# Four attentions of one kernel: 18 score tiles ahead of the loop in place of 24, three a step in the first six steps, and another place for the second norm

## What is computed

```python
x = x + _L0_attn_ref(_layernorm(x), ...)   # window and global tokens, ALiBi, rope, 8 key heads   -> stage a0
x = x + _L0_ffn_ref(_layernorm(x), ...)
x = x + _L1_attn_ref(_layernorm(x), ...)   # causal                                            -> stage a1
x = x + _L1_ffn_ref(_layernorm(x), ...)
x = x + _L2_attn_ref(_layernorm(x), ...)   # causal with rope                                  -> stage a2
x = x + _L2_ffn_ref(_layernorm(x), ...)
x = x + _L3_attn_ref(_layernorm(x), ...)   # full, heads mixed over batches                    -> stage a3
x = x + _L3_ffn_ref(_layernorm(x), ...)
```

## Time and profile before

| what | us |
|---|---|
| median of 3 runs | 1944.53 |
| lowest and highest | 1933.18, 1951.77 |
| the profiled execution | 1942.08 |
| its span | 1940.3 |
| PE busy in it | 1628.8 |
| DVE busy in it | 1179.9 |
| ACT busy in it | 865.3 |
| POOL busy in it | 477.8 |

### The profile page before, as it was taken

The page is one execution under the profiler, slowest core; times in us unless marked ns, Lnnn a source line. Parts: engine busy times, 40 slices in busy tenths (PEclk is TensorE's granted clock), DMA queues, the critical chain, the costliest instruction groups (busy, mean ns, idle before and its releaser), DMA issues. The chain is left out here.

```text
span 1940.3 us, 28833 instructions
## 1 busy us (share of the span) xinstructions
PE 1628.8 (84%) x10648; PEld 942.5 (49%) x10654; DVE 1179.9 (61%) x2595; ACT 865.3 (45%) x1360; POOL 477.8 (25%) x594
## 2 busy tenths in 40 slices
PE   4989999899999999911499999869998999998676
PEld 2334443478855556501245555546775344433433
DVE  2677777343255665469857676456454777775476
ACT  1255555433215555522025445437673366566322
POOL 4222210023213312030222330016664422210100
PEclk9789999999999999965699999969999999999798
DMA  7351350100064335010245424031113355140322
GB/s 244 81 130 52 85 135 2 66 1 0 1 182 126 94 87 153 2 50 0 70 124 152 123 64 120 1 123 50 50 50 93 110 126 150 36 120 1 118 88 88
DMA packets 68688, 162.29 MB, mean 84 GB/s; under 512 B 10013, under 2 KB 15526, under 8 KB 67562
## 3 DMA queue, kind: packets, MB, share of 16 engines
q1 hardware_dynamic: 68554, 160.52, 29.2%
HBM read 111.06 MB, written 53.09 MB: 85 GB/s over the span
## 5 line engine op out<-in xcount | busy, mean ns | idle before, releaser
L1079 DVE TENSOR_REDUCE a_mx<-PS 128x1 f32<-128x512 f32 (+3 forms) x768 | 395.0, 553 | 184.3 <-PE PS L1321 113.0
L1262 ACT ACTIVATE a_pT<-PS 128x1024 f32<-128x1024 f32 (+3 forms) x384 | 308.6, 811 | 222.4 <-PE PS L1345 154.5
L1316 PE MATMUL PS<-a_k,a_q 64*128 64x512 f32 (+3 forms) x768 | 228.6, 413 | 30.4 <-DVE a_mx L1079 24.5
L405 DVE CUSTOM_DVE_ANT_0 PS<-PS,a_dist 128x448 f32<-128x448 f32 x256 | 156.2, 642 | 59.6 <-PE PS L650 58.3
L1336 PE MATMUL PS<-a_q,a_k 64*128 64x512 f32 (+3 forms) x768 | 174.2, 433 | 6.2 <-issue 3.2
L1359 PE MATMUL PS<-a_pT,a_va 128*32 128x512 f32 (+3 forms) x1536 | 166.8, 506 | 5.7 <-ACT a_raw L1220 5.7
L122 PE MATMUL PS<-cst 128*128 128x512 f32 x248 | 131.1, 657 | 44.5 <-PEq L66 35.2
L555 ACT ACTIVATE a_pT<-PS 128x448 f32<-128x448 f32 (+1 forms) x256 | 123.5, 542 | 95.4 <-PE PS L673 95.0
L1316 PEld LDWEIGHTS PS<-a_k,a_q 64*128 64x128 f32 x768 | 105.7, 186 | 102.6 <-DVE a_mx L1079 87.8
L1336 PEld LDWEIGHTS PS<-a_q,a_k 64*128 64x128 f32 x768 | 77.2, 185 | 107.2 <-issue 78.5
L2046 POOL TENSOR_TENSOR f_h_low<-f_prod,f_h_high 128x512 fp32r<-128x512 f32 x84 | 110.2, 1318 | 60.2 <-ACT f_h_high L2233 57.8
(11 more groups left out here) (355 smaller groups left out, 3449.9 us busy)
## 6 DMA issues: line engine op xcount, KB each, us to landing
spread_scratch<-a_high SPq DMA_DIRECT2D x96, 256.0 KB, 7.3
a_q<-spread_scratch SPq DMA_DIRECT2D x96, 256.0 KB, 5.7
a_k<-spread_scratch SPq DMA_DIRECT2D x96, 256.0 KB, 6.4
f_gb<-gate_rows SPq DMA_DIRECT2D x68, 256.0 KB, 5.2
spread_scratch<-a_low SPq DMA_DIRECT2D x48, 256.0 KB, 7.8
a_q<-window_scratch SPq DMA_DIRECT2D x32, 256.0 KB, 5.4
a_k<-window_scratch SPq DMA_DIRECT2D x32, 256.0 KB, 6.3
window_scratch<-a_high SPq DMA_DIRECT2D x24, 256.0 KB, 3.5
```

What stands on the lines that cost most here:

```text
L405: dve.tensor_tensor_reduce(PS[:, 4 + a, 0:KW], PS[:, 4 + a, 0:KW], dt_[:, off:off + KW], 1.0, 3e38, ALU.add, ALU.min, mx[:, gg % 2, qt, 2 ...
L1079: dve.tensor_reduce(mx[:, gg % 2, qt, 2 * half + a:2 * half + a + 1], PS[:, 4 + a, 0:kw], AX.X, ALU.max).then_inc(max_done, 1)
L1262: act.activation(pT[:, N // 2 % 2, N % 2, :, q0:S], PS[:, 2 * (N % 2):2 * (N % 2) + 2, q0:S], ACT.Exp, scale=SCALE).then_inc(exp_done, 1)
L1316: mm = pe.matmul(ps[:, 0:kw], q[rows, b % 2, pair, qt * P:(qt + 1) * P], k[rows, b % 2, pair, 0:kw], start=True, stop=not causal)
```

## The change

The number of tiles ahead of the loop goes from 24 to 18 in all four attentions. The loop does three tiles in each of steps 0 to 5 and two from then on, so that from step 5 on the same tiles are done as before. `turn_maxima(0, 0)` comes after tile 17 in place of tile 19, with the `keep_busy` of 3 right behind it, and a0 gets that `keep_busy` too. In DVE's list the stats of the second norm go to behind unit 1's exchange where there is rope (in a1 and a3 they stay), and apply, and in a0 `total(1)`, go ahead of tile 0; a0's `sigmoid(1)` goes behind `keep_minima(0, 0)`. In POOL's list the norm's root goes between unit 1 and unit 2.

```diff
-    LEAD = 24
+    FIRST, LEAD = 18, 24
+        def scored(N):
+
+            return min(NB * TILES_, 2 * (N + 1) + LEAD, FIRST + 3 * (N + 1))
+
 (attention_window, POOL)
-                layer_norm_pool(pool, ln, 1, neg_half)
-                pool.wait_ge(ln.rstd_done, 2)
+                    if u == 1:
+                        layer_norm_pool(pool, ln, 1, neg_half)
+                pool.wait_ge(unit_low[NU - 1], 1)
                 pool.memset(pT[GLOB:P, 2, :, GLOB:S], 0.0).then_inc(ones_done, 1)
 (attention_window, DVE)
                     exchange(0, u)
-                layer_norm_stats(dve, ln, 1, source(1))
+                    if u == 1:
+                        layer_norm_stats(dve, ln, 1, source(1))
                 dve.wait_ge(loaded_dist, 16)
-                for t in range(8):
-                    minima(t)
                 dve.wait_ge(transposed, 2 * KC)
                 layer_norm_apply(dve, ln, 1, source(1))
-                for t in range(8, 4 * TB):
+                total(1)
+                for t in range(FIRST):
                     minima(t)
-                total(1)
-                for t in range(4 * TB, LEAD):
-                    minima(t)
+                keep_minima(0, 0)
                 sigmoid(1)
-                keep_minima(0, 0)
                 for N in range(FULL):
-                    for t in (2 * N + LEAD, 2 * N + LEAD + 1):
-                        if t < NB * TILES_:
-                            minima(t)
+                    for t in range(scored(N - 1), scored(N)):
+                        minima(t)
 (attention_window, PE)
-                for t in range(4 * TB + 4):
+                for t in range(FIRST):
                     scores(t)
                     if t % 2:
                         keep_busy(pe, PS, cst, 3, 1)
                 pe.wait_ge(va_done, 1)
                 turn_minima(0, 0)
-                for t in range(4 * TB + 4, LEAD):
-                    scores(t)
+                keep_busy(pe, PS, cst, 3, 3)
                 pe.wait_ge(masks_done, 2)
                 for N in range(FULL):
                     scores_T(N)
-                    for t in (2 * N + LEAD, 2 * N + LEAD + 1):
-                        if t < NB * TILES_:
-                            scores(t)
+                    for t in range(scored(N - 1), scored(N)):
+                        scores(t)
 (attention_quads, POOL)
                 if rope is not None:
-                    for u in range(NU):
+                    for u in range(2):
                         rotated(0, u)
                         lower(0, u)
                 layer_norm_pool(pool, ln, 1, neg_half)
+                if rope is not None:
+                    for u in range(2, NU):
+                        rotated(0, u)
+                        lower(0, u)
 (attention_quads, DVE)
                         exchange(0, u)
+                        if u == 1:
+                            layer_norm_stats(dve, ln, 1, source(1))
                 else:
...
-                layer_norm_stats(dve, ln, 1, source(1))
-                for t in range(4 * TB):
-                    maxima(t)
+                    layer_norm_stats(dve, ln, 1, source(1))
                 dve.wait_ge(transposed, KC)
                 layer_norm_apply(dve, ln, 1, source(1))
-                for t in range(4 * TB, LEAD):
+                for t in range(FIRST):
                     maxima(t)
                 keep_maxima(0, 0)
 (attention_quads, PE)
-                for t in range(4 * TB + 4):
+                for t in range(FIRST):
                     scores(t)
                     if t % 2:
                         keep_busy(pe, PS, cst, 3, 1)
                 pe.wait_ge(va_done, 2)
                 turn_maxima(0, 0)
-                for t in range(4 * TB + 4, LEAD):
-                    scores(t)
                 keep_busy(pe, PS, cst, 3, 3)
```

More of the change, by code:

```diff
@@ L1163, in _ @@
                 for N in range(FULL):
-                    for t in (2 * N + LEAD, 2 * N + LEAD + 1):
-                        if t < NB * TILES_:
-                            maxima(t)
+                    for t in range(scored(N - 1), scored(N)):
+                        maxima(t)
                     piece(*piece_at(N))
```

## The result

The kernel after is slower: 1956.8 us as the median of 16 runs, against 1939.16 for the kernel before on the same chips, a ratio of 1.0075 with a 95% interval of 1.0051 to 1.0100 (the ratio leaves out one slow run of after, at 1967.98, and is that of the means of the others, 1954.7 and 1940.1). The forecast was 1935.0, in a range of 1925 to 1948. The runs of after also scatter more (1935.1 to 1967.98; those of before 1933.18 to 1951.77). Their time goes with the mean granted clock of the whole execution: 1935.1 us at 0.930, the other fifteen 1946.0 to 1967.98 us at 0.923 to 0.909. The profiled execution took 1956.33 us, with a span of 1954.5.

The account below looks back on a forecast made before the run. No one engine bounds the kernel, though PE, 84% busy, leads in the loop's first steps. Gains of 5.0 + 1.8 + 1.7 + 1.0 = 9.5 us give 1932.6 profiled, 1935.0 median, range 1925 to 1948.

Parts of the forecast that it names:

- The entry: Tile 16 to the loop: takes 4.8 us in the new order, so the loops start earlier, together 17.3 us gained.
- The price of the owed tiles: Steps 0 to 5: third tiles wait for DVE, costing 3.8 us in a3, 2.4 in a1, 2.5 in a2, 4.8 in a0.
- the walk: Step-by-step sum of steps 0 to 5 with the old trace's durations; in a3 step 6 came at 14.1 us for 10.26.
- the clock: Rival, loop steps: DVE waits bring one slow stretch of 1.7 us per attention, a0's tiles stay slow; 1944 us, chance 0.2.
- two well-sized terms: The 17.3 us gained ahead of the loops, against the cost of the same 24 tiles issued inside steps 0 to 5.
- Third tiles at full price: Rival, steps 0 to 5: each third tile costs 1.17 us, 28.1 against 17.3 gained; 1955 us, chance 0.17.
- The slack: Rival, steps 0 to 5: the six steps hide the owed tiles, 17.3 to 20 us gained; 1926 us, chance 0.12.
- The norm's move: Second norm's apply (1.4 us) and a0's sum (1.2) go where DVE waits for the spread, costing nothing.
- The fall inside the keep-busy: a0 ahead of tile 0: the clock falls late and briefly after 3.9 us of idle, costing 2 us.
- the signs of "wrong": Profile after: step 6 at its old distance, a0's tiles at 0.70, a new slow stretch in steps 0 to 8, DMA wait.
- signs of "right": Profile after: entry 4.8 us, half-microsecond idle before third tiles, step 6 at 14, 12.8, 16 us, a0's tiles at 1.00.

Follow-up runs that it names:

- the late order: The kernel after with the third tile of steps 0 to 5 moved behind the step's values and piece in PE's list: 0.9970 of before.
- the runs with filler: The kernel after plus a useless 128 x 256 matmul ahead of third tiles: steps 0 to 5 0.9992, 0 and 1 0.9984, 2 to 5 0.9993 of before.
- the late order with filler: The kernel after with third tiles behind values and piece, plus one useless matmul in steps 0 and 1: 0.9954 of before.
- the fastest kernel: The kernel before with only the second norm's move, plus the triple keep-busy ahead of a0's loop: 0.9911 of before.
- the filler: The kernel after plus one useless 128 x 256 matmul, behind a wait for bank 7, ahead of the third tile of steps 0 to 5: 0.9992 of before.
- the twelve steps: The kernel after with the six owed tiles spread over twelve steps, one extra every second step: 1.0068 of before.
- the run without the entry filler: The kernel before with only the second norm's move, less the triple keep-busy before the loop of a1 to a3: 0.9949 of before.
- filler in steps 0 and 1: The kernel after plus the useless 128 x 256 matmul ahead of the third tile in steps 0 and 1 alone: 0.9984 of before.

## Why the prediction was wrong, step by step

- **The entry was right.** Tile 16 to `scores_T(0)` takes 4.5 to 4.6 us (4.8 forecast), and tile 0 to the loop gains 5.7, 4.4, 4.4 and 5.0 in a0 to a3, 19.5 in all, against 2.4 + 17.3 = 19.7 forecast. In a0 it is 5.7 of 6.5, with tiles 0 to 15 at a clock of 0.79 and not at the 1.00 of the forecast.
- **The price of the owed tiles was about right at full clock, and too low in a0.** To step 6 the walk had 2.4 in a1 and 3.8 in a3; to step 8 the late order measured 2.9 and 3.7. For a2 it had 2.5, and the runs with filler have 21.55 - 18.80 = 2.8 and 21.30 - 18.80 = 2.5. For a0 it had 4.8; the late order with filler needs 22.2 to step 8 where the fastest kernel needs 17.3: 4.9. The sum is 14.3 against the 13.5 of the walk. The plain order without any filler never ran wholly at full clock in a1 to a3, so its own price stays bracketed: in a1 between 2.7 (18.09 - 13.55, less four useless matmuls of some 0.46, half of what each of the triple takes) and 4.5, and at most 2.5 in a2 and 19.27 - 13.80 = 5.5 in a3. In a0 it nearly did: 25.0 - 17.3 = 7.7, of which the clock of 0.93 explains at most (1 - 0.93) x 25.0 = 1.8, so it costs 5.9 or more there.
- **The step that failed is the clock.** "I walked the steps with these durations", all of them at 2.4 GHz, and the fall had a place only as a rival, at "(1 - 0.87) x 13.43 = 1.7 us each" and a chance of 0.2. That size came from one short slow stretch in a2. The stretches of after last 20.5 to 23.9 us, and what they cost, step 8 less the full-clock price, is 9.4 - 2.9 = 6.5, 10.4 - 2.8 = 7.6 and 11.0 - 3.7 = 7.3: 21.4 us in three stages, four times the rival's 5.1 there. With the bounds of the plain order as the price, 4.5, 2.5 and 5.5, it is 18.3 at the least. Put 21.4 on the forecast of 1932.6 for the profiled execution and it is 1954.0; it took 1956.33. That this comes so close is in part luck, since the stages moved by up to 3.3 us behind step 8 too: a0 was 1.0 ahead there and 4.3 at its end.
- **The sign hung on it.** Gains at the entry (19.5) less full-clock price (14.3) leave 5.2, and the 20.3 - 17.3 = 3.0 that a0's steps give back at full clock make it 8.2, near the 9.5 forecast. Slow stretches of that size in two stages eat all of it, and there were three. A further 2.8 us went in a0, 25.0 - 22.2: partly in its short slow stretch, partly by the plain order of its list. The forecast balanced two well-sized terms and left out the one that was larger than their difference.
- **The other rivals.** Third tiles at full price gave 1955, near the measured time, by a mechanism that the runs refute as the main cause: the filler adds work to PE's list ahead of each third tile and still takes 4.4 to 7.4 us off in a1 to a3. Order has a smaller part, seen in a0 and in the twelve steps. The slack did not take them all: at full clock they cost 2.5 to 4.9 a stage or more. The page "TensorE: Matmul & The Clock Gate" of the Trainium skill, section "HAM oscillation — how this bites in real kernels", pointed to the right rival, though the waits that it describes are long ones for a DMA and here none was over 0.8 us; a1 and a3, which I set against it because they kept 1.00 through short waits in the kernel before, fell once the waits were more.
- **The norm's move was not free but a gain**, 0.5% alone. I counted it only in a0 and found 4.5 us from tile 0 to the loop (26.1 to 21.5), as forecast for the tiles at full clock. The fall inside the keep-busy that I expected is there (the clock averages 0.85 over 37.0 to 48.7 in the norm's move alone), but tile 0 came at 48.71, so the 2 us that I set aside for it were not paid. In the kernel after that stretch lies in the tiles instead, at 0.79. The other three entries gain 0.1, 0.1 and 0.6, which makes 5.3 of about 10. The profile of that run has fewer slow stretches elsewhere in a1 and a3, but such stretches come and go between runs of one kernel; where the rest comes from stays open.
- **What the profile after was to show**: of the signs of "wrong", the one that came is "an attention shows a new slow stretch in steps 0 to 8", in all of a1, a2 and a3. The signs of "right" that failed are step 6 (20.19, 18.50 and 21.85 us into the loops of a3, a1 and a2 for 14, 12.8 and 16) and the clock in a0's tiles 0 to 15 (0.79 for 1.00). Tile 32 waited for no DMA.

## What to carry to other kernels

Before moving work out of a stretch that PE shares with a slower engine, look at what PE has left to do there: here six tiles fewer in front and six waits more behind let the clock fall for 20 us in each of three stages, which cost some 21 us where 9.5 were to be gained. Price such a fall as one that may last, not by the short slow stretches that the kernel happens to show now. And where PE must wait, useless matmuls in the gap can be cheaper than none: one line of them ahead of a0's loop gave 3 us in the profile. They are no surety: with two of them added to the late order a3 lost its clock.

## What the runs showed of the hardware that I had not expected

- The clock fell with no idle stretch of PE longer than 0.8 us, after 3.7 to 6.1 us in which PE worked for 71 to 77% of the time (in the kernel before 82 to 98% over the same time from the loop's start, and no fall there). PE's busy share alone does not tell the cases apart: with the late third tile it worked 4.87 of the first 6.00 us of a1 and 2.72 of the first 3.68 of a3 and the clock stayed, and with filler in steps 0 and 1 5.73 of 6.00 in a1, and it fell later, in the steps without filler.
- Once down it stayed down for 20.5 to 23.9 us, with PE busy for 87 to 95% of that time. In the run without the entry filler, where nothing but two tiles a step followed and PE was busy for all of the stretch, it was back after 9.3 us.
- A slow stretch need not cost anything. At a clock of 0.76 over 18.84 us a2 lost nothing against 0.91 over 18.80, while a3 at 0.72 lost 2.7.
